# Four-layer conditioned sequence kernel: scale and shift behind the transposition, rows spread by DMA

## The chip, the cores and the metric

The kernel runs on one core of a Trainium2 chip. The metric is the device time of one execution in microseconds (us), less is better; the time of a version is the median of its timed executions.

## The reference, cut to what matters

Eight sequences of 256 tokens with 288 channels go through three transformer layers and one rotation. Every layer is conditioned: six vectors per sequence (shift, scale and gate, for attention and for the MLP) come from `silu(cond) @ W + b`. Layer 0 has a mixture of four experts as its MLP, layers 1 and 2 a plain one (288 to 1152 to 288). Layer 1's attention is between the 16 heads of one token, not between tokens.

```python
def block(x, c):                       # layers 0, 1, 2
    sh1, sc1, g1, sh2, sc2, g2 = split(silu(c) @ w_ada + b_ada, 6)
    h = layernorm(x) * (1 + sc1) + sh1
    x = x + g1 * attention(h)          # 16 heads of 18; layer 1: heads of one token attend to each other
    h = layernorm(x) * (1 + sc2) + sh2
    return x + g2 * mlp(h)             # layer 0: top 2 of 4 experts
U, _ = qr(P)                           # P is 288 x 64
R = expm(skew(silu(c) @ W.T + b))      # 64 x 64 for each sequence
x = x + ((x @ U) @ R - x @ U) @ U.T
```

## The kernel before, in words

X lies in SBUF as 16 tiles of 128 tokens x 288 channels (`X`); a block `b` is one sequence, two tiles. `XT` holds the transposed activations as fp16 pairs (high part and remainder), so that one fp32 product is seven fp16 matmuls (`PRODUCTS`, all issued by L1323). The MLP works on chunks of 512 tokens: `up_mm` has 63 matmuls of 512 columns, `down_mm` 112 of 288 columns, and an expert's weights are brought back from DRAM (`w_back`, tiles `W`, 1440 and 1368 KB) between two chunks.

A planner in Python sets the order. Generators (`prep`, `attend`, `settle_tokens`, `finish`, `householder`, `ada`, the MLP's `up` and `down`) hand out steps with `do(lane, kind, cost, ...)`; `deal` takes the line of best rank whose inputs should be ready by the planner's clock of TensorE (with the margin `SLACK`), and each engine then executes its steps strictly in that order, waiting on semaphores. `LANDS` is the time that a DMA is planned to take, `cost` that of a step; these numbers shape the order but not what hardware does. `copy` and `sooner` choose between ScalarE and VectorE, or GpSimd and VectorE. All DMAs but the loads of x are issued by SyncE (SP).

The parts that the change touches:

- **Layer norm** (`layernorm`, 48 times). VectorE makes mean and variance, GpSimd the factors, ScalarE writes z = (x - mean) * r into `YL` (`ln_z`). VectorE multiplies by the scale row (`ln_scale`, L1652), VectorE or GpSimd adds the shift row (`ln_shift`, L1657 or L2142), both rows read from `ADB`, which a DMA fills for every block with rows spread over 128 partitions. TensorE transposes (`xb_T`, L1343 and L1344), ScalarE writes the high parts (`x_hi`), VectorE the remainders (`x_lo`).
- **The QR of P** (`householder`) by 64 reflections, one after another. For each, TensorE spreads row j of `AT` over 64 partitions by an fp32 matmul with a column of the identity (`hh_mm`, L1493), ScalarE copies it into `BC` and sums its squares (`hh_row`, L2077 and L2079), GpSimd takes the root (`hh_root`, L2162), and VectorE makes ten instructions of the reflection (`hh_step`, L1857 to L1873). The line stands in the background chain `bg`, behind `ada(2)`. U is needed by the rotation after layer 2's MLP.
- **Layer 1's softmax sums** (`settle_tokens`, 8 times). VectorE takes reciprocals (`t_rec`, L1713), TensorE spreads them over partitions by 16 fp32 matmuls (`t_bc`, L1399), VectorE multiplies four times (`t_norm`, L1719) into `OT`, and `t_proj` (also L1323, tile `OT`) follows.

Of the kernel before, what the change touches and what calls it, by code (L numbers as in the profile page):

```python
# [24 lines left out]
LANDS = dict(w_back=6.0, w_keep=5.8, ad_in=3.9, ae_in=4.3, g2_in=4.0, x_in=7.5, w_in=5.0, w2_in=6.0, cond_in=5.0, tv_in=3.3)  # L25
AHEAD = 3
SLACK, BIAS = -0.3, 0.2
# [86 lines left out]
def slot(ring):  # L114
    return slots(ring, 1)


def two(ring):
    return slots(ring, 2)
# [15 lines left out]
def program(nc, I, out, scr_ada, scr_v, scr_o, scr_w1, scr_w2):  # L135
    ctx = ExitStack()
    with ctx:
# [29 lines left out]
        def mm_cost(n, cols, wide=1):  # L167
            return n * max(0.056, cols / 2350 * wide + 0.003)
# [18 lines left out]
        ADB = sb("ADB", [128, 10 * C])  # L187
        AD1 = [ADB[:, 2 * i * C:(2 * i + 2) * C] for i in range(2)]
        AD2 = [ADB[:, (4 + 3 * i) * C:(7 + 3 * i) * C] for i in range(2)]
# [7 lines left out]
        KB = [sb(f"KB{i}", [128, NH, 64], F16) for i in range(2)]  # L197
        SAME = sb("SAME", [128, 8], F16)
# [35 lines left out]
        N2 = sb("N2", [D, 2])  # L234
# [43 lines left out]
        rE, rE1, rTM, rG, rOS, rSTG = Ring([0, 1]), Ring(range(4)), Ring([0, 1]), Ring([0, 1]), Ring([0, 1]), Ring(range(7))  # L278
# [20 lines left out]
        def cond_rows(w, bias, n, dst, plus, name, wide):  # L299
            w_v = w.rearrange("(k p) n -> p k n", p=96)  # L300
            stores, total = [], n // C
            for k in range(0, total, wide):
# [17 lines left out]
                s = do(sp, "cond_out", 0.1, raises=f"os{o}", incs=16 * len(some), o=o, dst=tuple(dst[:, (k + g) * C:(k + g + 1) * C] for g in some), src=a)  # L320
                rOS.free[o] = [s]
                stores = [x for x in stores if x.sem is not s.sem] + [s]
# [5 lines left out]
        def split_cols(dst, before, w, cols, scales, bias, eager=False):  # L328
# [8 lines left out]
            for blk in range(3):  # L337
# [5 lines left out]
                for a, b, s in scales:  # L343
# [111 lines left out]
        def to_columns(b, y, full, mixed=False):  # L455
# [15 lines left out]
        def layernorm(w, L, b, sc, sh, rows, mixed=False, ask=None):  # L471
# [16 lines left out]
            while (("ada", L), 1) not in tok:  # L488
                yield "wait"
# [1847 lines left out]
```

## Time and profile before

| | |
|---|---|
| median of 3 runs | 1620.38 us (1617.28 to 1622.78) |
| profiled execution, its own time | 1614.11 us |
| span of the profiled execution | 1612.3 us |
| TensorE (PE) busy | 1391.3 us, 86% |
| VectorE (DVE) busy | 1004.1 us, 62% |
| ScalarE (ACT) busy | 787.7 us, 49% |
| GpSimd (POOL) busy | 412.9 us, 26% |
| mean granted TensorE clock | 0.94 |

PE's time is the sum of its busy time and its idle time; an idle stretch is put down to what ended it. PE is busiest, so a stage is read by asking which wait ends last on PE.

### The profile page before, as it was taken

The numbers are of one execution on the slowest core, as the hardware profiler recorded it, in microseconds if no ns is written. First come the engines' busy times: TensorE is split into PE (matmuls) and PEld (weight loads), VectorE is DVE, ScalarE is ACT, GpSimd is POOL, SyncE is SP. The second block draws the span as 40 slices with busy tenths as digits, with TensorE's granted clock in tenths as the row PEclk, the third lists the DMA queues.
The fourth block names the chain that finished last, engine by engine and source line by source line (L and its number), as shares of the span: only waits on it lengthen the run. The fifth ranks groups of instructions, "written<-read, shape, count | busy, mean of one in ns | idle before, by whom it ended". The sixth has DMA issues, their size and how long they took to land.

```text
span 1612.3 us, 30341 instructions
## 1 busy us (share of the span) xinstructions
PE 1391.3 (86%) x11814; PEld 826.6 (51%) x11814; DVE 1004.1 (62%) x2361; ACT 787.7 (49%) x1534; POOL 412.9 (26%) x551
## 2 busy tenths in 40 slices
PE   3667988988899989899898987898998899899977
PEld 1333554544455555555455554464554456565634
DVE  4676766467585666566574766856647687766442
ACT  2553545656475434454343544555444465555522
POOL 1011314133332332233231332323413131231100
PEclk9788989999999999999999999899999899999968
DMA  6232234443122210221212212230011010000010
GB/s 174 63 120 76 75 106 143 138 137 107 62 60 70 84 68 19 71 77 58 80 30 91 57 73 87 56 78 20 27 42 49 28 54 26 24 13 9 27 38 15
DMA packets 80389, 106.09 MB, mean 66 GB/s; under 512 B 39469, under 2 KB 67318, under 8 KB 76918
## 3 DMA queue, kind: packets, MB, share of 16 engines
q1 hardware_dynamic: 78134, 101.79, 20.6%
q10 hardware_dynamic: 2112, 2.36, 0.5%
q8 instruction: 94, 1.54, 0.4%
q14 instruction: 49, 0.40, 0.1%
HBM read 87.37 MB, written 16.49 MB: 64 GB/s over the span
## 4 chain that ended last, share of the span: by engine, by line
PE 51%; DVE 19%; issue 12%; DMA 6%; ACT 5%; POOL 5%; SPq 2%; POOLq 0%; DVEq 0%; ACTq 0%
PE P L1323 21%; DVE NM L1737 4%; PE P L1476 4%; PE P L1477 4%; PE P L1478 4%; PE P L1445 3%; PE P L1436 2%; PE P L1343 2%; DMA QT<-MT 1%; PE P L1412 1%; POOL N L2162 1%; POOL X L2147 1%; PE P L1333 1%; DVE AT L1869 1%; DMA STG<-in_L_b 1%
## 5 line engine op out<-in xcount | busy, mean ns | idle before, releaser
L1323 PE MATMUL P<-XT,W 128*128 128x512 f16 x1512 | 356.3, 387 | 14.4 <-DVE NM L1737 6.2
L2147 POOL TENSOR_TENSOR X<-X,TM 128x288 f32<-128x288 f32 x144 | 121.9, 847 | 716.4 <-DVE TM L1812 480.5
L1476 PE MATMUL P<-W,H 128*128 128x288 f16 x864 | 254.6, 295 | 1.9 <-POOL H L2152 1.8
L1477 PE MATMUL P<-W,H 128*128 128x288 f16 x864 | 254.1, 294 | 0.0
L1478 PE MATMUL P<-W,H 128*128 128x288 f16 x864 | 253.9, 294 | 0.0
L1323 PEld LDWEIGHTS P<-XT,W 128*128 128x128 f16 x1512 | 142.9, 99 | 193.5 <-issue 25.1
L2061 ACT ACTIVATE ARENA<-P 128x512 f32<-128x512 f32 x256 | 137.8, 602 | 131.8 <-PE P L1436 131.4
L2071 ACT ACTIVATE G<-P 128x512 f32<-128x512 f32 x216 | 128.4, 594 | 109.8 <-PE P L1323 99.9
L1737 DVE TENSOR_REDUCE NM<-P 128x2 f16<-128x512 f32 x256 | 160.3, 687 | 1.4 <-PE P L1421 0.5
L2152 POOL TENSOR_TENSOR H<-G,H 128x512 f16<-128x512 f32 x98 | 121.8, 1248 | 133.2 <-ACT H L2072 132.8
L1323 PE MATMUL P<-WQ,XT 128*128 128x288 f16 x1008 | 151.6, 303 | 4.2 <-issue 3.1
L1806 DVE TENSOR_TENSOR H<-G,H 128x512 f16<-128x512 f32 x118 | 85.4, 728 | 69.1 <-ACT H L2072 68.7
L2072 ACT ACTIVATE H<-P 128x512 f16<-128x512 f32 x216 | 128.1, 593 | 0.0
L1323 PEld LDWEIGHTS P<-WQ,XT 128*128 128x128 f16 x1008 | 97.4, 103 | 49.5 <-issue 17.9
L1476 PEld LDWEIGHTS P<-W,H 128*128 128x128 f16 x864 | 86.8, 100 | 31.0 <-issue 6.3
L1478 PEld LDWEIGHTS P<-W,H 128*128 128x128 f16 x864 | 86.9, 101 | 24.3
L1477 PEld LDWEIGHTS P<-W,H 128*128 128x128 f16 x864 | 86.9, 101 | 23.8
L1986 ACT ACTIVATE XT<-P 128x512 f16<-128x512 f32 (+1 forms) x80 | 43.5, 554 | 111.5 <-PE P L1344 111.2
L2077 ACT ACTIVATE HQS<-P 64x288 f32<-64x288 f32 (+31 forms) x64 | 24.0, 375 | 131.1 <-PE P L1493 131.1
L1812 DVE SCALAR_TENSOR_TENSOR TM<-P,CW,G 128x288 f32<-128x288 f32 x64 | 32.7, 511 | 74.3 <-PE P L1478 74.2
L1445 PE MATMUL P<-ARENA,V 128*32 128x256 f32 x1024 | 71.7, 395 | 4.7 <-ACT ARENA L2061 4.5
L1436 PE MATMUL P<-QT,KT 64*128 64x256 f16 x512 | 52.2, 285 | 24.5 <-DMA QT<-MT 22.9
(293 smaller groups left out, 2266.0 us busy)
## 6 DMA issues: line engine op xcount, KB each, us to landing
W<-scr_w SPq DMA_DIRECT2D x9, 1440.0 KB, 6.2
W<-scr_w SPq DMA_DIRECT2D x9, 1368.0 KB, 5.8
ADB<-scr_ada SPq DMA_DIRECT2D x24, 432.0 KB, 3.9
ADB<-scr_ada SPq DMA_DIRECT2D x24, 288.0 KB, 4.8
scr_w<-W SPq DMA_DIRECT2D x4, 1440.0 KB, 5.9
scr_w<-W SPq DMA_DIRECT2D x4, 1368.0 KB, 5.0
STG<-in_L_w SPq DMA_DIRECT2D x10, 432.0 KB, 3.4
STG<-in_L_w SPq DMA_DIRECT2D x7, 576.0 KB, 5.0
```

What stands on the lines that cost most here:

```text
L1323: ins = e.matmul(o, l, r, start=k == 0, stop=k == len(pairs_) - 1)
L1445: ins = e.matmul(bank(st)[32 * i:32 * i + 32, at], V32[u][:, kt, 4 * g + i, :], E32[s][:, i, kt * 256:(kt + 1) * 256], start=kt == 0, stop ...
L1476: e.matmul(o, hi, W2[:, 2 * m, :], start=False, stop=False)
L1477: e.matmul(o, hi, W2[:, 2 * m + 1, :], start=False, stop=False)
L1478: ins = e.matmul(o, lo, W2[:, 2 * m, :], start=False, stop=m == 8)
L1737: e.tensor_reduce(NM[:, :, st["par"], st["c"]], bank(st).rearrange("p (n k) -> p n k", n=2), AX.X, ALU.max, negate=True).then_inc(st.sem)
L1806: e.tensor_tensor(H[:, m, 1, :], G32[st["gi"]][:, :], H[:, m, 0, :], ALU.subtract).then_inc(st.sem)
L2061: e.activation(E32[st["s"]][:, st["h"], :], bank(st), ACT.Exp).then_inc(st.sem)
L2071: e.activation(G32[st["gi"]][:, :], bank(st), fn, scale=1.0 / WS)
L2072: e.activation(H[:, st["m"], 0, :], bank(st), fn, scale=1.0 / WS).then_inc(st.sem)
L2147: e.tensor_tensor(X[:, t, :], X[:, t, :], TM[st["k"]][:, :], ALU.add).then_inc(st.sem)
L2152: e.tensor_tensor(H[:, m, 1, :], G32[st["gi"]][:, :], H[:, m, 0, :], ALU.subtract).then_inc(st.sem)
```

## The change

Scale and shift move behind the transposition. z itself is transposed; channels are then partitions, so scale and shift are one value per partition: `full` (three instructions on ScalarE or VectorE) reads PSUM and writes `FULL`, `m_hi` makes the high part from it, `m_lo` (VectorE or GpSimd) the remainder. The values come from `SC`, which `cond_T` (three small transposes for each pair of column groups, 27 in all) and `cond_cols` fill once for every layer. The 48 loads of `ADB` become 24 loads of one gate row (`G1`). A reflection's row is spread by a DMA from SP (`hh_row`), GpSimd makes five instructions of the reflection and VectorE four; the line gets a place of its own from the start. Layer 1's reciprocals go to `RCP` and are spread by 16 DMAs from SP (`t_spread`). The remainder and the bias remainder of a weight's last rows are one instruction (`w_lo3`). The planner's constants change too. The chunks of the MLP are as before.

```diff
-LANDS = dict(w_back=6.0, w_keep=5.8, ad_in=3.9, ae_in=4.3, g2_in=4.0, ...)
-SLACK, BIAS = -0.3, 0.2
+LANDS = dict(t_spread=3.5, w_back=6.0, w_keep=5.8, g1_in=3.3, g2_in=4.0, ...)
+SLACK, BIAS = -0.41, 0.01
-            return n * max(0.056, cols / 2350 * wide + 0.003)
+            return n * max(0.058, cols / 2240 * wide + 0.003)
...
-            s = do(dve, "ln_scale", 0.76, w=w, sc=sc, src=z, rows=rows or ask())
-            r = do(lane, "ln_shift", cost, raises=f"ln_shift_{lane.name}", w=w, sh=sh, src=s)
-            yield from to_columns(b, YL[w], r, mixed)
+            m = do(pe, "xb_T", 0.8, y=YL[w], js=(j, j2), full=z, free=[pf, pf2])
+            f = copy("full", 1.1 + BIAS, 1.15, L=L, b=b, sc=sc, sh=sh, mixed=mixed, i=i, js=(j, j2), src=m, cols=cols, free=ff)
+            hi = copy("m_hi", 0.95 + BIAS, 0.75, b=b, i=i, src=f, free=before)
+            lane, cost = sooner([hi], (pool, 2.5), (dve, 1.35))
+            lo = do(lane, "m_lo", cost, raises=f"m_lo_{lane.name}", ...)
...
             r = do(dve, "t_rec", 1.75, ...)
-                    m = do(pe, "t_bc", 0.55, c=c, i=kr, j=j, src=r, free=jf)
-                    outs.append(do(dve, "t_norm", 0.6, c=c, i=raw, j=j, src=m, ...))
+            bc = do(sp, "t_spread", 0.6, incs=256, i=kr, src=r, free=ef)
+            for c in range(4):
+                outs.append(do(dve, "t_norm", 0.5, c=c, i=raw, kr=kr, rows=bc, ...))
...
-                m = do(pe, "hh_mm", mm_cost(1, C - j, 4) + 0.1, c=j, j=c, src=last, free=pf)
-                a = do(act, "hh_row", 0.55, incs=2, c=j, j=c, src=m, free=last if j else None)
-                p = do(pool, "hh_root", 0.67, src=a, half=hp)
-                d = do(dve, "hh_step", 2.3, incs=10, c=j, src=a, root=p, at=p_in)
+                r = do(sp, "hh_row", 0.1, incs=16, c=j, src=last)
+                a = do(act, "hh_norm", 0.5, c=j, src=r)
+                p = do(pool, "hh_root", 2.0, incs=5, c=j, src=a, half=hp, free=last if j else None)
+                d = do(dve, "hh_step", 1.4, incs=4, c=j, src=a, root=p, at=p_in)
...
-        bg = Line(chain(n0, ..., ada(1), ada(2), skew(), householder(), expm_steps()), 3)
+        bg = Line(chain(n0, ..., ada(1), ada(2), skew(), expm_steps()), 3)
-        deal([loads, attends, ends_, tops, preps, bg, ...])
+        deal([Line(householder(), 4), loads, attends, ends_, tops, preps, bg, ...])
...
+            def t_spread(st):
+                q.wait_ge(st["src"], st["free"])
+                for s in range(4):
+                    for c in range(4):
+                        e.dma_start(spread_of(st["i"], c)[32 * s:32 * s + 32, :], RCP[32 * s + c:32 * s + c + 1, :].unsqueeze(1).broadcast_to([1, 32, 256])).then_inc(st.sem, 16)
+            def hh_row(st):
+                q.wait_ge(st["src"])
+                e.dma_start(BC[:, c:C], AT[c:c + 1, c:C].unsqueeze(1).broadcast_to([1, D, C - c])).then_inc(st.sem, 16)
```

How the order of instructions moves is shown at three places. One reflection on VectorE, before (the first of 64; HQS holds the spread row, HS single values, TI a pivot, N a norm):

```order
L1857 ISA HQS,HS<-HQS,AT 64x288
L1857 ISA HS 64x1
L1858 TENSOR_SCALAR HS<-HQS 64x1
L1860 SCALAR_TENSOR_TENSOR HS<-HS,N 64x1
L1862 SCALAR_TENSOR_TENSOR TI<-HS,HQS,N 64x1
L1864 RECIPROCAL HS<-TI 64x1
L1865 SCALAR_TENSOR_TENSOR HS<-AT,HS 64x1
L1867 SCALAR_TENSOR_TENSOR HS<-HS,NMK 64x1
L1869 SCALAR_TENSOR_TENSOR AT<-HQS,HS,AT 64x288
L1871 SCALAR_TENSOR_TENSOR AT<-HS,AT 64x1
L1873 SCALAR_TENSOR_TENSOR AT<-IDF,HS,AT 64x1
```

And now, a reflection of length 237 with its neighbours, the reciprocals of layer 1's third block among them (RCP); six of the ten steps have gone to GpSimd or away:

```order
L1879 ISA HQS,HS<-HQS,AT 64x237
L1879 ISA HS 64x1
L1881 RECIPROCAL HS<-TI 64x1
L1883 SCALAR_TENSOR_TENSOR HS<-HS,NMK 64x1
L1885 SCALAR_TENSOR_TENSOR AT<-HQS,HS,AT 64x237
L1735 RECIPROCAL RCP<-P 128x256
```

SP's queue around a reload of layer 0's weights in the first half of layer 1, before (W<-scr_w is the reload, QT<-MT a row of maxima that the attention scores wait for):

```order
L2219 DMA W<-scr_w 128x5760 [waits s_up_mm]
L2261 DMA QT<-MT 1x16x128 [waits s_tq_dve,s_t_top_out]
L2261 DMA QT<-MT 1x16x128
L2227 DMA ADB<-scr_ada 128x864 [waits s_proj_gate,s_ln_shift_dve]
L2219 DMA W<-scr_w 128x5472 [waits s_down_mm]
```

And now: the reflections' rows (HQS<-AT) and the 16 issues of a spread (ARENA<-RCP) stand ahead of the reload and of QT<-MT:

```order
L2321 DMA HQS<-AT 64x1x251 [waits s_hh_step]
L2321 DMA HQS<-AT 64x1x250 [waits s_hh_step]
L2321 DMA HQS<-AT 64x1x249 [waits s_hh_step]
L2309 DMA ARENA<-RCP 32x1x256 [waits s_t_av,s_t_rec]
L2309 DMA ARENA<-RCP 32x1x256 x15
L2265 DMA W<-scr_w 128x5472 [waits s_down_mm]
L2303 DMA QT<-MT 1x16x128 [waits s_tq_act,s_tq_dve,s_t_top_out]
```

TensorE behind the last attention product of layer 1's third block (ARENA,V and ARENA,EV), before; the spread stands as ARENA,IDF, and the projection of OT soon behind it:

```order
L1388 MATMUL P<-ARENA,V_0 32x128 x4
L1391 MATMUL P<-ARENA,EV 32x256 x4
L1323 MATMUL P<-WQ,XT 128x288 x14
L1323 MATMUL P<-XT,W 128x512 x7
L1399 MATMUL P<-ARENA,IDF 32x256 x16
L1356 MATMUL P<-IDH,QB 64x128 x16
L1323 MATMUL P<-WP,OT 128x288 x4
L1356 MATMUL P<-IDH,KB 64x128 x16
```

And now, for the fourth block, whose projection comes soonest: ahead of the rows shown, 56 of the `down_mm` matmuls (the last one is the first row) stand between its last attention product and OT; the spread has left TensorE:

```order
L1496 MATMUL P<-W,H 128x288
L1342 MATMUL P<-XT,W 128x512 x7
L1342 MATMUL P<-WP,OT 128x288 x8
L1342 MATMUL P<-XT,W 128x512 x35
L1369 MATMUL P<-IDF,ARENA 128x128 x2
```

## Rows read from the trace of the kernel before

**Rows 1.** The page: busy time, share and instructions of each engine.

```profile
PE 1391.3 (86%) x11814; PEld 826.6 (51%) x11814; DVE 1004.1 (62%) x2361; ACT 787.7 (49%) x1534; POOL 412.9 (26%) x551
```

**Rows 2.** Stretches: length, busy (x) PE PEld DVE ACT POOL, clock, DMA share, GB/s.

```profile
0.00:200.00 200.00, 132.30 (x1095) 72.17 (x1096) 126.17 (x263) 87.61 (x162) 33.64 (x67) 0.88 0.34 101
...
400.00:1000.00 600.00, 541.63 (x4525) 323.37 (x4523) 369.84 (x1037) 281.15 (x589) 175.00 (x222) 0.98 0.21 66
1000.00:1500.00 500.00, 447.61 (x4189) 274.11 (x4189) 337.95 (x736) 263.00 (x501) 134.76 (x176) 0.94 0.12 35
```

**Rows 3.** Waits of PE: line, what it waited for, us, times, longest.

```profile
PE P L1493 <- DVE AT L1873: 33.7, 26, 4.3
...
PE P L1436 <- DMA QT<-MT: 22.9, 8, 4.1
PE P L1378 <- DMA QT<-MT: 15.0, 6, 4.8
PE P L1421 <- DVE NM L1737: 14.9, 17, 2.7
...
PE P L1323 <- DVE OT L1719: 7.6, 6, 5.4
...
PE P L1343 <- POOL ARENA L2142: 5.6, 3, 2.9
...
PE P L1343 <- DVE ARENA L1657: 3.4, 2, 2.0
```

**Rows 4.** Groups by line, the reflections: busy us, mean ns, idle before and releasers.

```profile
L2162 POOL TENSOR_TENSOR N<-N,HP 64x1 f32<-64x1 f32 x64 | 42.2, 660 | 65.1 <-ACT HQS L2079 65.0
L1493 PE MATMUL P<-AT,IDF 64*64 64x288 f32 (+42 forms) x128 | 41.7, 406 | 35.7 <-DVE AT L1873 33.7 <-DVE NM L1700 1.3 <-ACT ARENA L2061 0.6
...
L1857 DVE CUSTOM_DVE_ANT_0 HQS<-HQS,AT 64x288 f32<-64x288 f32 (+31 forms) x64 | 30.8, 482 | 21.9 <-ACT HQS L2079 21.3
...
L1860 DVE SCALAR_TENSOR_TENSOR HS<-HS,N 64x1 f32<-64x1 f32 x64 | 21.5, 336 | 28.9 <-POOL N L2162 25.8
...
L1873 DVE SCALAR_TENSOR_TENSOR AT<-IDF,HS,AT 64x1 f32<-64x1 f32 x64 | 13.5, 210 | 2.3
```

**Rows 5.** Groups by line: the spread of reciprocals and its neighbours.

```profile
L1399 PE MATMUL P<-ARENA,IDF 128*32 128x256 f32 x256 | 15.9, 383 | 1.2 <-DVE ARENA L1713 1.2
...
L1719 DVE TENSOR_TENSOR OT<-P,ARENA 128x256 f32<-128x256 f32 x32 | 15.3, 591 | 5.7 <-PE P L1399 5.5
...
L1713 DVE RECIPROCAL ARENA<-P 128x256 f32<-128x256 f32 x8 | 14.0, 1747 | 0.0
```

**Rows 6.** Groups by line: the layer norm's parts and its transposes.

```profile
L1343 PE MATMUL P<-IDF,ARENA 128*128 128x128 f32 x256 | 50.0, 291 | 16.5 <-POOL ARENA L2142 5.6 <-DVE NM L1737 4.0 <-DVE ARENA L1657 3.4
...
L2142 POOL TENSOR_TENSOR ARENA<-ARENA,ADB 128x576 f32<-128x576 f32 x32 | 48.4, 1514 | 71.3 <-DVE ARENA L1652 71.2
...
L1652 DVE TENSOR_TENSOR ARENA<-ARENA,ADB 128x576 f32<-128x576 f32 x48 | 36.9, 770 | 14.6 <-ACT ARENA L1993 10.7 <-DMA ADB<-scr_ada 3.9
```

**Rows 7.** SP's queue in order of time: start, us, DMA issues.

```profile
533.49 1.15 SPq L2261 DMA_DIRECT2D QT<-MT  x2
...
848.60 0.33 SPq L2219 DMA_DIRECT2D W<-scr_w  x1
852.18 1.14 SPq L2261 DMA_DIRECT2D QT<-MT  x2
```

**Rows 8.** The chain that ended last: start, us, piece.

```profile
144.87 1.76 DMA QT<-MT
...
518.52 1.62 PE P L1323 x7
...
537.56 0.12 PE P L1477
...
852.73 2.68 DMA QT<-MT
```

**Rows 9.** DMA issues by line: count, KB each, median us to landing.

```profile
W<-scr_w SPq DMA_DIRECT2D x9, 1440.0 KB, 6.2
```

More of the change, by code:

```diff
@@ L319, in cond_rows @@
                 yield [a]
[L320 to L322 removed]
+                last = []
+                some = [g for g in some if L is None or k + g in (2, 5)]
+                if some:
+                    last.append(do(sp, "cond_out", 0.1, raises=f"os{o}", incs=16 * len(some), o=o, gs=tuple(some), dst=tuple(dst[:, (k + g) * C:(k + g + 1) * C] for g in some), src=a))
+                    stores = [x for x in stores if x.sem is not last[0].sem] + last
+                if L is not None:
+                    yield from slot(rP)
+                    _, j, pf = rP.take()
+                    m = do(pe, "cond_T", 0.4, o=o, n=32 * len(bufs), j=j, src=a, free=pf)
+                    rOS.free[o] = last + [m]
+                    yield [m]
+                    c = do(act, "cond_cols", 0.65, L=L, k=k, n=len(bufs), j=j, src=m)
+                    rP.free[j] = [c]
+                    for g in range(len(bufs)):
+                        tok["cols", L, k + g] = c
+                else:
+                    rOS.free[o] = last
                 for g in some:
@@ L885, in finish @@
                 ot_rd[0] = ms_
[L886 to L887 removed]
+            g1_rd[u] = [v]
+            yield from layernorm(1, L, b, 4, 3)
             if L == 0:
@@ L1853, in hh_step @@
                 j = st["c"]
-                bc, aj, a1 = BC[:, j:C], AT[:, j:C], AT[:, j:j + 1]
-                nb, sg, g, rt, w, d = (HS[:, k:k + 1] for k in range(6))
-                q.wait_ge(st["src"], st["at"], (st.sem, st.first) if st.first else None)
-                e.tensor_tensor_reduce(out=HQ[:, j:C], in0=bc, in1=aj, scale=1.0, scalar=0.0, op0=ALU.mult, op1=ALU.add, accum_out=d).then_inc(st.sem)
-                e.tensor_scalar(sg, bc[:, 0:1], 0.0, 2.0, ALU.is_ge, ALU.mult).then_inc(st.sem)
@@ L1866, in hh_step @@
-                q.wait_ge(consts, st.at(6))
-                e.scalar_tensor_tensor(out=g, in0=w, scalar=rt, in1=NMK[:, j:j + 1], op0=ALU.mult, op1=ALU.mult).then_inc(st.sem)
-                q.wait_ge(st.at(7))
+                bc, aj = BC[:, j:C], AT[:, j:C]
+                g, rt, w = (HS[:, k:k + 1] for k in range(3))
+                q.wait_ge(st["src"], st["at"], st["root"].at(4), (st.sem, st.first) if st.first else None)
+                e.tensor_tensor_reduce(out=HQ[:, j:C], in0=bc, in1=aj, scale=1.0, scalar=0.0, op0=ALU.mult, op1=ALU.add, accum_out=w).then_inc(st.sem)
```

300 lines of the change are left out of this document (164 added, 136 removed).

## Prediction

> **What bounds the kernel now.** I read the page's first part, then stretches, then PE's waits, then groups by line. TensorE is busy for 1391.3 of 1612.3 us and no other engine for more than 62% [rows 1], so the time is PE's busy time plus 221.0 us of PE's idle time. The stretches say where the idle time lies [rows 2]: 67.7 of the first 200 us, 58.4 of the 600 us in which layer 0's experts run beside layer 1, 52.4 of the 500 us behind them. An engine off PE only matters where PE waits for it. The largest such waits inside the kernel are for the reflections (33.7 us in 26 waits), for the row of maxima QT<-MT that SP sends (22.9 and 15.0), for the row maxima on VectorE (14.9), for OT (7.6), and for the shift of the layer norm (5.6 and 3.4) [rows 3].
>
> **What leaves PE.** The 64 fp32 matmuls of the reflections keep PE busy for 41.7 us, and it idles 33.7 us for them, since each can only start when VectorE has finished the last reflection [rows 4]. The work goes altogether: **-41.7**. Of the waits I take **-30.0**: in a full MLP stretch the next matmul is ready, but some waits will turn into a wait for something else. Bounds: -33.7 if none does, -17 if half do. The 128 matmuls (256 in the trace) that spread the reciprocals are 15.9 us of PE [rows 5]: **-15.9**. What comes to PE is 27 small transposes; the nearest row is L1343, 50.0 us for 256 [rows 6], 0.195 us each: **+5.3** (none would be the lower bound, twice as much the upper).
>
> **The layer norm.** Before, VectorE multiplies (0.77 us) and VectorE or GpSimd adds (as much, or 1.51 us) ahead of the transposes [rows 6]. That is 1.5 to 2.3 us of latency which goes. `full` comes in behind the transposes, three instructions; the trace has none like it, and the nearest is L1719 with 0.59 us for 128x256 [rows 5], so at most 1.8 us, on VectorE 14 times and ScalarE 34 times. A layer norm's chain so changes by +0.3 us at the worst, and by about -1.1 if `full` takes 1.2. Of the 9.0 us that PE waited for the shift [rows 3] I take **-6**; bounds -9.0 and +5. VectorE is relieved on the whole: six of the instructions of a reflection, L1860 with 336 ns and L1873 with 210 among them [rows 4], are 64 x 6 x 0.21 to 0.34 = 81 to 129 us, and L1652 another 36.9 [rows 6], while part of `full` and `m_hi` comes in. With some 100 of 1004 us gone from VectorE, a third of PE's wait for the row maxima, 14.9 us [rows 3], should go: **-5** (bounds 0 and -14.9). GpSimd gets four more small instructions per reflection: at most 64 x 4 x 0.66 = 169 us by L2162 [rows 4], less the 48.4 of L2142 [rows 6]. It is 26% busy [rows 1]; that is its cover, and I put it at nothing.
>
> **The spread of the reciprocals, now on SP.** The plan counts 0.6 us for the issue of 16 DMAs and 3.5 for landing. But two SBUF-to-SBUF issues took 1.15 us [rows 7], 0.57 each, so the 16 hold SP for 9.1 us, and the last lands 1.76 later, as QT<-MT did [rows 8]: 10.9 us in place of 4.1, eight times. Then come VectorE's four products. From the last attention product to a ready OT it is 1.75 + 9.1 + 1.76 + 4 x 0.59 = 15.0 us [rows 5, 7, 8]. In PE's order 56 `down_mm` matmuls of 0.12 us and seven `up_mm` of 1.62 together stand between for the fourth block [rows 8]: 8.3 us, so PE stops for 6.7. The sixth block stands alike; together 13.4. For the third and fifth block 28 and 49 such matmuls stand between, 14.7 us, about enough; for the others more. Queued behind the stuck `t_norm` on VectorE are the remainders `h_lo` and the gates `down_gate`, for which ScalarE's gelu and PE's banks wait: I add half a microsecond a block, 4 us. Queued behind the spread on SP are reloads of W and QT<-MT. **+17**; bounds 0 (all hidden) and 87 (8 x 10.9, nothing hidden).
>
> **The rows of the reflections, now on SP.** A row costs SP 0.57 us and 1.76 to land, and a reflection's round gets longer than before (GpSimd's five in a row are up to 5 x 0.66). That alone costs nothing: 64 rounds of even 10 us are 640, the line starts at once, and U is needed only behind layer 2's first MLP chunk. What costs is the order. Each row waits on SP for VectorE's last reflection, with loads behind it; and ScalarE (`hh_norm`) and GpSimd (`hh_root`) wait in order for the row to land, with gelu and the additions to X behind them. In SP's order 13 of the 64 rows stand directly behind a reload or a save of 1.4 MB. A reload takes 6.2 us [rows 9]; QT<-MT, issued 3.6 us behind one [rows 7], landed after 2.68 rather than 1.76 [rows 8], that is, with the reload's end (848.60 + 6.2 = 854.8 against 855.4). A row issued at once behind a reload should so come 4.4 us late. 13 x 4.4 = 57 us is the upper bound; PE has up to seven other banks to fill meanwhile, so I take about a sixth: **+9** (lower bound 0).
>
> **The start.** P's load and the first rows stand in SP's queue among the first loads, with some `w_adaln` columns behind them, while the round trip of scale and shift through DRAM is gone. I see no sign of either winning and put it at nothing, within 5 us. The merged `w_lo3` lies beside other work.
>
> **The sum**, against the profiled execution's own time: 1614.1 - 41.7 - 30.0 - 15.9 + 5.3 - 6 - 5 + 17 + 9 = 1546.8 us. The median of the runs is 6.3 above that execution (1620.4), and I carry that over: **1553 us**.
>
> **The rivals.**
>
> *A: the new waits stay hidden and the old ones vanish.* The spread and the rows cost nothing, all 33.7, 9.0 and 14.9 us of waits go: 1614.1 - 41.7 - 33.7 - 15.9 + 5.3 - 9.0 - 14.9 + 6.3 = 1510 us. For it: PE has MLP matmuls in reserve in most of the 600 us stretch, where its clock is already 0.98 [rows 2]. Against it: the same was so for QT<-MT, whose waits still cost 37.9 us [rows 3], with an issue and landing only a little longer than planned.
>
> *B: the rows behind a reload cost in full.* ScalarE stops 4.4 us at each of 13 places and gelu is what PE is waiting for in an `up_mm` stretch. The sum then has 57 in place of 9: 1601 us. For it: the one crossing that rows 7 and 8 show. Against it: a reload of W1 is followed by `down_mm`, in which ScalarE has little to do.
> The Trainium skill ("DMA: Bandwidth & Descriptors", section "Queues, rings and completion order") says that on each DMA engine descriptors are consumed in ring order, which is B's mechanism; the crossing in rows 7 and 8 agrees with it, 855.4 against 854.8.
>
> *C: slower, by SP's queue.* With 192 new issues of 0.57 us, 109 us, less the 24 loads saved, SP's queue gets full, and each row in it waits for VectorE. QT<-MT, V and the reloads stand behind. Each of the 24 attentions waits for QT<-MT, and the price falls on PE at once, as rows 3 show. The gain of 67 us is used up from 67 / 24 = 2.8 us more at each; at 4 us more it is 1553 + 96 = 1649 us. Against it: most of SP's time it waits for other engines, and only 4 of the QT<-MT pairs have a reflection's row directly ahead.
>
> *D: no effect to speak of.* The 100 us off PE's path are replaced by waits of the same size, because something behind PE (the planner's order as a whole) sets the pace: 1610 to 1620 us. For it only that the order of every engine changes.
>
> **Chances.** Forecast (1525 to 1580) 0.58, A 0.18, B 0.13, C 0.06, D 0.05. The measurement can tell about 0.3%, 5 us, from no change. Faster by more than that: 0.58 + 0.18 + 0.13 + a part of D = 0.91; same 0.03; slower 0.06. The range that leaves out C, D and the outer parts of A and B is 1508 to 1600 us.
>
> **What would show it.** PE busy at about 1391.3 - 41.7 - 15.9 + 5.3 = 1339 us, VectorE near 900, GpSimd above 450. No waits of PE for reflections. On SP 16 issues in a row of about 9 us in all, and behind them PE's wait for OT of 6 to 7 us in layer 1's fourth and sixth block; a spread that takes 4 us says that this term was wrong. ScalarE idle for 4 us ahead of a reflection's squares, behind a reload, with PE idle behind it, is B. PE's wait for QT<-MT far above 37.9 us is C. The forecast is wrong, too, if PE's idle time, 221 before, isn't near 1547 - 1339 = 208 less the 2 us around the span: then a stage that I hold for unchanged, the start above all, has changed.

## The result, and the profile after

The changed kernel takes **1643.06 us** (median of 4 runs, 1641.87 to 1645.18), the kernel before 1619.84 in the same comparison: a ratio of 1.0144, with a 95% interval from 1.0123 to 1.0166. It is 1.4% slower where 1553 us was forecast. Its profiled execution has a span of 1640.2 us at a mean granted clock of 0.912, against 1612.3 us and 0.940 before.

The page's first part, which answers to [rows 1]:

```profile
PE 1326.4 (81%) x11457; PEld 811.6 (49%) x11457; DVE 872.0 (53%) x1908; ACT 816.3 (50%) x1581; POOL 426.1 (26%) x802
```

TensorE's work went down as forecast, to 1326.4 us (1339 was worked out), and VectorE's to 872.0 (near 900). GpSimd's 426.1 is less than the 450 that I had named. But the idle time of TensorE, 1640.2 - 1326.4 = 313.8 us, is 92.8 more than before, where 208 was expected. The stretches, against [rows 2]:

```profile
core 0: us, PE busy (x) PEld busy (x) DVE busy (x) ACT busy (x) POOL busy (x), PEclk, DMA share, GB/s
0.00:200.00 200.00, 122.78 (x1009) 64.98 (x1010) 127.77 (x295) 94.41 (x194) 45.31 (x124) 0.84 0.36 84
200.00:400.00 200.00, 171.47 (x1473) 103.56 (x1471) 123.64 (x270) 123.71 (x237) 66.69 (x126) 0.95 0.46 125
400.00:1000.00 600.00, 481.25 (x4472) 305.94 (x4470) 278.71 (x634) 258.84 (x515) 158.06 (x310) 0.91 0.38 60
1000.00:1500.00 500.00, 433.25 (x3641) 267.16 (x3641) 281.20 (x582) 273.44 (x509) 136.65 (x213) 0.93 0.20 39
```

In the 600 us in which layer 0's experts run beside layer 1, TensorE is busy for 481.3 us instead of 541.6: 60 us lost there. The first 200 us lost 9.5, the next 200 some 4 and the 500 from 1000 us on 14. The granted clock of the long stretch is 0.91, where it was 0.98. TensorE's waits, against [rows 3]:

```profile
engine line waited for: us in total, times, longest us
PE P L1342 <- DVE OT L1741: 109.4, 7, 19.3
PE P L1439 <- DVE NM L1759: 26.5, 14, 15.0
```

The first row alone is more than the 92.8 us by which the idle time grew: the projection of layer 1 waits for OT for 109.4 us in seven waits, up to 19.3 long, one in each of the first seven blocks. Before it was 7.6 [rows 3]. In the eighth block TensorE waits for something else, 15.0 us for the row maxima NM (the longest wait of the second row). The reason is the same, since it is VectorE that stands still. Its first product waits for the spread in every one of the eight blocks, and whatever stands behind that product in VectorE's order waits with it:

```profile
DVE OT L1741 <- DMA ARENA<-RCP: 121.5, 8, 16.6
```

The waits for the reflections (33.7) and those of layer 1's scores for QT<-MT (15.0) are gone; the other waits for QT<-MT are about as before (24.7 against 22.9).

How one such wait comes about, the first block's, is seen in three timelines (start, duration, then engine and line). SP's issues:

```profile
547.88 15.49 SPq L2309 DMA_DIRECT2D ARENA<-RCP  x16
```

VectorE's reciprocals and its first product:

```profile
545.98 1.75 DVE L1735 RECIPROCAL RCP<-P 128x256 f32<-128x256 f32 x1
...
567.69 0.59 DVE L1741 TENSOR_TENSOR OT<-ARENA 128x256 f32<-128x256 f32 x1 [15.45 <-DMA ARENA<-RCP]
```

and TensorE's projection:

```profile
570.22 4.02 PE L1342 MATMUL P<-WP,OT 128*128 128x288 f32 x8 [13.93 <-DVE OT L1741]
```

The reciprocals are ready at 547.73. SP then issues 16 DMAs for 15.49 us, 0.97 each, and the product starts at 567.69: 20.0 us for what I had put at 10.9. TensorE ran out of other work 13.93 us before the projection. What such an idle stretch does to the work behind it shows in the granted clock, third from the end in these rows of the idle stretch and of the 5 us behind it:

```profile
556.00:570.00 14.00, 0.29 (x3) 0.00 (x0) 2.31 (x5) 0.00 (x0) 0.00 (x0) 0.65 0.83 119
570.00:575.00 5.00, 4.78 (x32) 3.12 (x32) 0.97 (x3) 1.09 (x2) 0.98 (x2) 0.61 0.08 32
```

It is 0.65 on average in the idle stretch, so the lower of the two levels (1.2 GHz) was granted for most of it, and still 0.61 in the busy 5 us behind it. The eight projection matmuls there take 4.02 us; the next eight, at 579 us, take 2.21. All 128 take 48.8 us, 36.5 before:

```profile
L2020 ACT ACTIVATE FULL<-P,SC 128x256 f32<-128x256 f32 (+1 forms) x102 | 49.2, 555 | 22.6 <-PE P L1370 22.4
L1342 PE MATMUL P<-WP,OT 128*128 128x288 f32 x128 | 48.8, 545 | 109.4 <-DVE OT L1741 109.4
...
L2111 ACT ACTIVATE HQS<-HQS 64x288 f32<-64x288 f32 (+31 forms) x64 | 26.5, 414 | 222.8 <-DMA HQS<-AT 222.6
```

The other rows here are new pieces: `full` takes 0.55 us an instruction, the columns' transposes 4.0 us of TensorE in all, and ScalarE sat idle for 222.6 us ahead of the reflections' squares, waiting for rows.

The two new kinds of DMA, each with its issues and its time from issue to landing. The spread:

```profile
L2309 SPq DMA_DIRECT2D ARENA<-RCP x128: 502/1093/1395, 547.9 to 1202.4; - x128
...
DMA to landing us min/median/max: 3.3/5.5/6.9
```

The row of a reflection:

```profile
L2321 SPq DMA_DIRECT2D HQS<-AT x64: 463/484/1249, 16.8 to 1084.8; - x64
...
DMA to landing us min/median/max: 3.7/4.1/5.7
```

### The profile page after: what moved, and what is told of

The parts are those of the page before. It is cut to its first block, busy times and chain, and to the rows that moved or that the text cites. A ratio compares the mean times of both kernels' runs of the same rounds, so it can differ in the third digit from the quotient of the medians.

```text
span 1640.2 us, 29488 instructions
## 1 busy us (share of the span) xinstructions
PE 1326.4 (81%) x11457; PEld 811.6 (49%) x11457; DVE 872.0 (53%) x1908; ACT 816.3 (50%) x1581; POOL 426.1 (26%) x802
## 4 chain that ended last, share of the span: by engine, by line
PE 50%; issue 12%; DVE 9%; DMA 9%; SPq 9%; ACT 6%; POOL 4%; POOLq 0%; DVEq 0%; ACTq 0%
PE P L1342 25%; SPq L2309 7%; PE P L1494 4%; PE P L1495 4%; PE P L1496 4%; DMA HQS<-AT 4%; PE P L1463 3%; DVE NM L1759 2%; PE P L1454 2%; PE P L1369 2%; DMA ARENA<-RCP 2%; PE P L1430 2%; POOL X L2185 1%; ACT FULL L2020 1%; PE P L1359 1%
## 5 line engine op out<-in xcount | busy, mean ns | idle before, releaser
L2190 POOL TENSOR_TENSOR H<-G,H 128x512 f16<-128x512 f32 x95 | 114.9, 1212 | 165.9 <-ACT H L2106 156.9
L1342 PE MATMUL P<-WQ,XT 128*128 128x288 f16 x1008 | 144.4, 295 | 9.5 <-ACT WQ L1987 6.6
L2111 ACT ACTIVATE HQS<-HQS 64x288 f32<-64x288 f32 (+31 forms) x64 | 26.5, 414 | 222.8 <-DMA HQS<-AT 222.6
L1342 PE MATMUL P<-WP,OT 128*128 128x288 f32 x128 | 48.8, 545 | 109.4 <-DVE OT L1741 109.4
L1342 PEld LDWEIGHTS P<-WP,OT 128*128 128x128 f32 x128 | 32.0, 259 | 123.0 <-DVE OT L1741 112.3
L1439 PE MATMUL P<-KT,QT 64*128 64x256 f16 x512 | 48.2, 289 | 46.1 <-DVE NM L1759 26.5
L1879 DVE CUSTOM_DVE_ANT_0 HQS<-HQS,AT 64x288 f32<-64x288 f32 (+31 forms) x64 | 28.5, 445 | 106.1 <-POOL HQS L2206 65.3
```

The costliest lines, as they stand in the source:

```text
L1342: ins = e.matmul(o, l, r, start=k == 0, stop=k == len(pairs_) - 1)
L2190: e.tensor_tensor(H[:, m, 1, :], G32[st["gi"]][:, :], H[:, m, 0, :], ALU.subtract).then_inc(st.sem)
```

## The experiments

Each kernel is a change of the changed kernel, or of the one before, as its diff says. e1 to e4 have 1615.9 us as the kernel before's median, e5 to e8 1620.9, e9 to e12 1617.9, e13 to e16 1618.3, e17 and e18 1618.2. All ratios are against it. e14, the changed kernel with the old cost constants, gave no time.

### Which part is it (e1 to e4)

**e1**: the reciprocals go back to TensorE, all else as in the changed kernel.

```
-            bc = do(sp, "t_spread", 0.6, incs=256, i=kr, src=r, free=ef)
...
+                    m = do(pe, "t_bc", 0.55, c=c, i=kr, j=j, src=r, free=jf)
...
+                    outs.append(do(dve, "t_norm", 0.6, c=c, i=raw, j=j, src=m, ...
```

> Of the changed kernel one part is undone: the reciprocals of layer 1 are spread by TensorE's t_bc again, as before. Theory S (the spread by 16 DMAs is what was mis-sized): TensorE's 109.4 us of waits for OT fall back to about 8, and 15.9 us of t_bc come back: 1643 - 101 + 16 = 1558 us, 1545 to 1575. Theory R (the reflections' rows on SP's queue cost as much): it stays at 1600 or above, and the idle time turns up ahead of the banks that ScalarE frees. Theory T (the start and the lower clock are losses of their own): between, 1575 to 1600, with the granted clock still near 0.91.

Measured: 1557.58 us, ratio 0.9629 (0.9602 to 0.9655), within a microsecond of theory S. Its stretches and its wait for OT:

```profile
0.00:200.00 200.00, 122.02 (x1006) 64.34 (x1007) 127.11 (x293) 94.29 (x194) 45.53 (x124) 0.83 0.36 84
...
400.00:1000.00 600.00, 554.23 (x5097) 352.32 (x5095) 321.03 (x724) 291.70 (x577) 191.32 (x374) 0.97 0.29 67
```

```profile
PE P L1349 <- DVE OT L1756: 12.0, 5, 5.0
```

The 600 us stretch has 554.2 us of TensorE work again and OT costs 12.0. So the spread alone costs 1643.1 - 1557.6 = **85.5 us**, and without it the change makes the kernel faster. The start is not better: 122.0 us in the first 200, as in the changed kernel.

**e2**: of the change only scale and shift behind the transposition are left, with the merged `w_lo3` and the new cost constants (e1's diff, and with it `hh_mm`, the old `hh_row`, `hh_root` and `hh_step`, in the background line).

> Of the changed kernel only scale and shift behind the transposition is left (with the small merges that go with it); reciprocals and reflections are as before. My sum for this part was +5.3 - 6 - 5: about 1615 us, 1605 to 1620. Theory T (the layer norm's new chain and the start lose time): 1625 or above. Against e1 it gives the price of the reflections: by the sum 63 us more than e1.

Measured: 1587.61 us, 0.9815 (0.9791 to 0.9839). This part is worth 28 us, not 6, and the reflections by DMA on top of it (e1) 30, not 63. Two waits of TensorE say where some of the missing 33 us are: for QT<-MT, behind SP's queue, 42.6 us in e1 and 28.2 in e2, and for the layer norm's z from ScalarE (`xb_T` for `ln_z`), 18.6 and 5.8.

**e3**: the kernel before with the reflections' part alone.

```
-                m = do(pe, "hh_mm", mm_cost(1, C - j, 4) + 0.1, c=j, j=c, src=last, free=pf)
...
-                d = do(dve, "hh_step", 2.3, incs=10, c=j, src=a, root=p, at=p_in)
+                r = do(sp, "hh_row", 0.1, incs=16, c=j, src=last)
...
+                d = do(dve, "hh_step", 1.4, incs=4, c=j, src=a, root=p, at=p_in)
...
-        deal([loads, attends, ...
+        deal([Line(householder(), 4), loads, attends, ...
```

> The kernel before with one part of the change: the rows of the reflections by DMA, four steps on VectorE, a line of their own. Sum: 1620 - 41.7 - 30 + 9 = 1557 us (1545 to 1575) if the parts add up. Theory R (rows stuck behind reloads stop ScalarE and so TensorE): 1600 or more.

Measured: 1642.82 us, 1.0159 (1.0136 to 1.0182): slower by 27 us, though all reflections' work is off TensorE. Its first stretches:

```profile
0.00:200.00 200.00, 109.13 (x934) 59.05 (x935) 130.68 (x303) 79.64 (x168) 43.96 (x135) 0.80 0.44 100
200.00:400.00 200.00, 164.27 (x1335) 92.94 (x1334) 137.00 (x289) 107.48 (x208) 65.71 (x116) 0.91 0.44 116
```

109.1 and 164.3 us stand against 132.3 and 175.6 in [rows 2]: 34 us are lost by 400 us. The wait for the layer norm's shift (L1650) is 22.9 us, where it was 3.4 and 5.6 on its two engines [rows 3].

**e4**: the changed kernel with only the reflections undone.

> The changed kernel with only the reflections undone (by TensorE and in the background line, as before). Theory S: e2 plus what the spread costs, some 85 us net of the t_bc saved, about 1700 us. If spread and reflections hurt each other on SP's queue, it costs clearly less here than between e1 and the changed kernel: 1660 or below.

Measured: 1666.84 us, 1.0312 (1.0287 to 1.0338). Spread on top of e2 costs 79 us, on top of e1 85.5: nearly the same with and without reflections' rows on the queue. (The 1700 expected was 85 on top of the 1615 expected for e2.) But the waits for OT are only 36.2 us here, 23 more than e2's 13.3:

```profile
PE P L1514 <- DVE AT L1903: 61.1, 33, 13.8
PE P L1345 <- DVE OT L1749: 36.2, 5, 12.0
...
PE P L1433 <- DVE QB L1695: 14.3, 1, 14.3
PE P L1396 <- DVE TM L1842: 13.5, 1, 13.5
PE P L1497 <- DVE H L1836: 12.9, 1, 12.9
```

VectorE waits for the spread as long as in the changed kernel, 115.1 us in eight waits. TensorE, though, often comes first to something else that stands behind the stuck product in VectorE's order: a reflection (twice, 13.2 and 13.8 us; in e2 no wait for one is over 3.4), the queries' remainder QB, the gates' product TM, the MLP's H. So where the plan does not know the spread's length, its price is the time for which VectorE stands still, and the wait for OT is only the most frequent form of it.

### Where the reflections' rows cost (e5, e6)

Why is the start worse with them? SP's first issues in e1:

```profile
17.14 0.51 SPq L2336 DMA_DIRECT2D HQS<-AT  x1
17.69 0.59 SPq L2246 DMA_DIRECT2D H<-in_L_w_adaln  x1
...
67.12 0.75 SPq L2294 DMA_DIRECT2D QT<-MT  x1
```

and in e2:

```profile
6.38 0.42 SPq L2254 DMA_DIRECT2D H<-in_L_w_adaln  x1
...
52.25 0.74 SPq L2302 DMA_DIRECT2D QT<-MT  x1
```

In e1 the first row waits on SP for P, whose load was issued 10.5 us earlier (6.60), and the next load of `w_adaln` goes at 17.69 instead of 6.38. The later rows wait on SP for VectorE's last reflection, the third one for 21.2 us, and the load of `w_proj` behind it goes at 52.65, in e2 at 39.78. The first QT<-MT goes at 67.12 instead of 52.25. In e3 the wait for P is not what costs, since the same `w_adaln` load goes at 20.35 there and at 19.64 in the kernel before; the loads behind the later rows are late (`w_gate` at 52.04 against 34.91).

**e5**: e1 with the reflections in the background line again, their rows still by DMA.

```
-        deal([Line(householder(), 4), loads, ...
+        bg = Line(chain(..., skew(), householder(), expm_steps()), 3)
```

> e1 (TensorE spreads the reciprocals) with one more edit: the reflections, rows still by DMA, go back into the background line behind skew, so that the first row no longer waits on SP for P ahead of a load of w_adaln. Theory Q (the rows cost where they stand in SP's and ScalarE's order at the start, 15 us at the first QT<-MT and some 24 us of TensorE work by 400 us): 1557.6 less 15 to 24, 1534 to 1543 us, and the first 200 us hold about 137 us of TensorE work as in e2, not 122. Theory V (the rows cost as much anywhere): within 5 us of e1, 1553 to 1562.

Measured: 1567.07 us, 0.9672 (0.9633 to 0.9712): no better than e1, somewhat worse. Its stretches show both halves:

```profile
0.00:200.00 200.00, 135.87 (x1177) 76.19 (x1178) 129.69 (x282) 103.25 (x196) 34.46 (x73) 0.87 0.28 79
...
1500.00:1561.00 61.00, 48.60 (x486) 34.88 (x481) 24.98 (x53) 13.46 (x34) 3.18 (x4) 0.99 0.11 40
```

The start is repaired as expected (135.9 us, and 176.6 in the next 200: 21 more than e1). But reflections that start at 410 us end at 1376 and not at 1006, and the matrix exponential, a chain of small fp32 matmuls, is left for the end: 486 matmuls in the last 61 us, where e1 has 223 in its last 57. The gain is given back; that the late end is what takes it is my reading, no run changes it alone.

**e6**: the same edit to e3.

> e3 (the kernel before with the reflections by DMA) with the reflections in the background line behind skew again. Theory Q: the 23 and 11 us of TensorE work missing in the first two stretches of e3 come back and the 27 us loss turns into a gain: 1643 - 34 = 1609 or less, down to 1575. Theory V: stays at 1635 to 1650.

Measured: 1585.04 us, 0.9776 (0.9748 to 0.9805): 58 us less than e3, by moving one line of work. There the reflections' part is worth 36 us instead of costing 27.

### What the spread's price is made of (e7, e8, e17, e16)

**e7**: the same 512 rows of 1 KB in 4 DMAs instead of 16.

```
-                for s in range(4):
-                    for c in range(4):
-                        e.dma_start(spread_of(st["i"], c)[32 * s:32 * s + 32, :], RCP[32 * s + c:32 * s + c + 1, :].unsqueeze(1).broadcast_to([1, 32, 256]))...
+                for c in range(4):
+                    src = RCP[c:128:32, :].unsqueeze(1).broadcast_to([4, 32, 256])
+                    e.dma_start(spread_of(st["i"], c), src).then_inc(st.sem, 16)
```

> The changed kernel with the same bytes and the same 1 KB rows of the spread, in 4 DMAs to 128 partitions each in place of 16 to 32. Theory I (each issue costs about 1 us, 15.5 us for 16): the issues take 2 to 4 us and the last lands 5.5 later, 9 us in place of 21, and the time falls by some 70 us to about 1575. Theory P (the engines need that long for 512 rows of 1 KB out of four partitions, and the queue only holds SP back): first issue to last landing stays at 16 to 21 us, and the time at 1625 to 1645.

Measured: 1584.36 us, 0.9774 (0.9751 to 0.9797). SP's issues and VectorE's reciprocals and first product:

```profile
549.49 5.27 SPq L2309 DMA_DIRECT2D ARENA<-RCP  x4
```

```profile
547.59 1.75 DVE L1735 RECIPROCAL RCP<-P 128x256 f32<-128x256 f32 x1
...
562.13 0.59 DVE L1741 TENSOR_TENSOR OT<-ARENA 128x256 f32<-128x256 f32 x1 [8.28 <-DMA ARENA<-RCP]
```

The 4 issues take 5.3 us, not 15.5, and the product starts 12.8 us after the reciprocals (549.34 to 562.13) instead of 20.0. TensorE's wait for OT is 55.8 us. 7.2 us less in each of eight places is 58, and 59 us are gained. So theory I holds in its main part, but an issue costs 1.3 us here, and the product starts 7.4 us after the end of the issues and not 5.5. Where the time goes shows in the share that the 16 DMA engines are busy (next to last column), here in e7 between 552 and 556 us, while nothing else moves much:

```profile
552.00:556.00 4.00, 4.00 (x102) 3.27 (x101) 0.69 (x1) 2.09 (x6) 0.00 (x0) 1.00 0.23 51
```

and the same in the changed kernel:

```profile
552.00:556.00 4.00, 4.00 (x69) 3.00 (x62) 0.24 (x1) 0.48 (x3) 0.00 (x0) 1.00 0.83 29
```

With 16 DMAs the engines are busy for 0.83 and move 29 GB/s; with 4 they are busy for 0.23 and move 51. The changed kernel's DMA view of a stretch in which only a spread runs, 1146 to 1158 us, has the packets:

```profile
DMA packets 525, 0.38 MB, mean 31 GB/s; under 512 B 173, under 2 KB 524, under 8 KB 524
...
q1 hardware_dynamic: 524, 0.36, 80.0%
```

0.80 x 16 x 12 = 154 us of engine time for 351 packets of 1 KB and 173 short ones: up to 0.44 us for a packet of 1 KB. In e7's 4 us above it is 0.23 x 16 x 4 = 14.7 us for 203 packets, 0.07 us each. That issuing is slow because the engines behind it are is my reading: the shortest issue takes 0.50 us and the median 1.09, and no run separates the two. The Trainium skill ("DMA: Bandwidth & Descriptors", section "Why a DMA increments its semaphore by 16 and not by 1") says that a DMA is spread over the largest number of engines, up to 16, that divides the slowest dimension of both sides. By that rule I estimate 16 for a spread of one row to 32 partitions and 4 for e7's (4 x 32 rows to 128 partitions). The shares agree with it: 0.83, and 0.23 where 4 of 16 can give 0.25 at most. So fewer engines spread the rows faster. Why a packet out of a single partition is so slow on 16 engines is not shown by these runs.

**e8**: the changed kernel, its plan told the truth.

```
-            bc = do(sp, "t_spread", 0.6, incs=256, ...
+            bc = do(sp, "t_spread", 15.5, incs=256, ...
-LANDS = dict(t_spread=3.5,
+LANDS = dict(t_spread=5.0,
```

> The changed kernel, the same instructions, but the plan that sets the order counts 15.5 us for issuing the spread and 5 for landing (it counted 0.6 and 3.5). Theory H (it is latency that an order can hide): the waits for OT fall from 109 to under 40 us, about 1575 us (1560 to 1600). Theory N (layer 1 has too little beside the spread, and SP's loads stand behind it): 1625 or more.

Measured: 1631.32 us, 1.0068 (1.0041 to 1.0095): 12 us back of 85. VectorE no longer stands still at the product (0.8 us in all), yet TensorE still waits 56.3 us for OT, since the spread itself is as long as before, and something else stands there, too:

```profile
PE P L1342 <- DVE OT L1741: 56.3, 5, 14.9
PE P L1342 <- ACT H L2106: 30.5, 4, 14.9
```

Its origin is in SP's order at one such place:

```profile
736.45 15.41 SPq L2309 DMA_DIRECT2D ARENA<-RCP  x16
751.91 1.21 SPq L2265 DMA_DIRECT2D W<-scr_w  x1
...
756.60 9.08 SPq L2321 DMA_DIRECT2D HQS<-AT  x2
```

and in ScalarE's order:

```profile
761.92 0.41 ACT L2111 ACTIVATE HQS<-HQS 64x244 f32<-64x244 f32 x1 [22.15 <-DMA HQS<-AT]
```

VectorE ends a reflection at 741.84. Its row is queued on SP behind the spread (until 751.86), a reload, two QT<-MT and the gates' rows, goes at 756.60 and lands at 761.9. ScalarE, in order, waits for it for 22.15 us with the gelus behind, and TensorE waits 14.7 for H. That is rival B's mechanism, behind the spread instead of behind a reload.

**e17**: e4 (no reflections' rows on SP) with the plan told 14 and 5 us.

> e4 (spread by 16 DMAs, reflections on TensorE) with the plan told 14 us of issue and 5 of landing. In e8 the same truth gave the changed kernel only 12 us, and two new waits of 15 us for ScalarE's H stood behind reflection rows held up by the spread. If that coupling is what ate the gain, then here, without such rows, it is larger: 1666.8 falls by 30 us or more, to 1637 or below. If layer 1 merely has too little work beside the spread: 1650 to 1665.

Measured: 1627.57 us, 1.0060 (1.0044 to 1.0076), 39 us less than e4 and more than three times what e8 gained. That is what was expected if the coupling with the rows ate the gain in e8; since the order is another one, too, it is no proof. TensorE's waits for OT, 36.2 us in e4, are gone, and so are the single waits of 13 to 14 us for VectorE, but it still is 40 us above e2. The largest wait is that of `hh_mm` for VectorE's reflection, 60.7 us in 39 waits, none over 3.9. It was 61.1 in e4 and 30.0 in e2: with the spread the reflections are late in either plan.

**e16**: e10 (below) with e7's form of the spread, planned with 5.2 and 4.8 us.

> e10 with the reciprocals by DMA again, in 4 DMAs as in e7, and the plan told their measured 5.2 us of issue and 4.8 of landing. If a latency of 12 us in place of 20 can be hidden once it is planned for: the 16 us of t_bc are saved, 1525 to 1540. If not, waits for OT of 40 to 56 us remain as in e7: 1560 to 1580.

Measured: 1564.64 us, 0.9676 (0.9662 to 0.9691), 25.5 us more than e10. VectorE waits 37.3 us for the spread, TensorE 19.4 for OT (11.9 in e10), and QT<-MT, 32.6 us in e10, now has 64:

```profile
PE P L1456 <- DMA QT<-MT: 42.4, 11, 8.5
PE P L1406 <- DMA QT<-MT: 21.4, 4, 8.2
```

The best form of the spread that I tried, in a plan that knows it, still loses to 16 us of matmuls. The longer waits for QT<-MT, which SP issues, fit SP's queue as the reason.

### How much is the order alone (e9 to e13, e15, e18)

**e9**: e1, with the reflections in a line of their own that starts when layer 0's block 3 has its q and k.

```
             last = p_in
+            while ("qk", 0, 3) not in tok:
+                yield "wait"
             for j in range(D):
```

> e1 with the reflections in their own line as there, but the first row waits in the plan until layer 0's block 3 has its q and k. The start should be e5's (135.9 and 176.6 us of TensorE work in the first two stretches, against 122.0 and 169.4 in e1), and the reflections should still end early enough that the matrix exponential is not left for the end, as it was in e5 (486 matmuls in the last 61 us, against 223). Theory Q: e1 less the 15 to 21 us of the start, 1537 to 1546 us. Theory V (the gain at the start is given back wherever the rows run): 1553 to 1562.

Measured: 1589.50 us, 0.9831 (0.9803 to 0.9858). Neither theory: 32 us worse than e1.

**e12**: the same from block 2 on.

> As e9, but from layer 0's block 2 on: some 40 us earlier. Theory Q: within 5 us of e9, since the start has been freed by then. If rows among the weight loads of layer 0 are what costs: 5 us or more above e9.

Measured: 1548.14 us, 0.9577 (0.9553 to 0.9602): 41 us better than e9 for a start one block earlier.

**e10**: e9, and the plan counts 4.3 us for a row's landing.

```
-LANDS = dict(t_spread=3.5,
+LANDS = dict(hh_row=4.3, t_spread=3.5,
```

> e9, with the plan counting 4.3 us for a row of the reflections to land (2.2 before; the trace has 4.0). If ScalarE's and GpSimd's waits for rows in order (184 us idle on ScalarE in e1) stop work that TensorE needs, the longer figure gives better places: 5 to 10 us less than e9. If not: within 4 us of e9.

Measured: 1539.10 us, 0.9515 (0.9493 to 0.9536): 50 us better than e9, by one number in the plan, and more than the 5 to 10 expected.

**e18**: e12 with the same number.

> e12 with the plan counting 4.3 us for a row to land, as e10 does to e9 (there 50 us less). If the longer figure is what helps: 10 us or more below e12's 1548, near 1535. If e9 was only an unlucky order: within 8 us of e12.

Measured: **1511.43 us**, 0.9342 (0.9316 to 0.9367), 37 us better than e12. The number helps at both places. What it does shows in ScalarE's waits for rows. e9 and, with the number, e10:

```profile
ACT HQS L2128 <- DMA HQS<-AT: 181.7, 36, 10.8
```

```profile
ACT HQS L2128 <- DMA HQS<-AT: 96.0, 18, 8.2
```

e12 has 170.1 us in 36 waits, and with the number, e18:

```profile
ACT HQS L2128 <- DMA HQS<-AT: 104.6, 19, 11.0
```

36 waits become 18 or 19, and their time falls from 170 to 182 us to about 100. The rows land after 4.0 us in all four. A plan that knows this seems to put other work of ScalarE ahead of an instruction that waits for a row, so that half of the waits are gone. e18 is the fastest version found, 6.6% below the kernel before. Its TensorE is busy for 1326.2 us, as long as the changed kernel's though it spreads the reciprocals as well (at a mean granted clock of 0.948 against 0.912), and idle for 1510.7 - 1326.2 = 184.5. Of the 600 us stretch it is busy for 561.1, at a clock of 0.98:

```profile
400.00:1000.00 600.00, 561.11 (x5157) 359.74 (x5158) 322.16 (x713) 294.87 (x580) 182.08 (x355) 0.98 0.31 73
```

**e11**: e2 with the plan's cost constants of the kernel before (slack, bias, the prices of a matmul and of `o_T`, MLP pieces, L3_WT's columns).

```
-SLACK, BIAS = -0.41, 0.01
+SLACK, BIAS = -0.3, 0.2
-            return n * max(0.058, cols / 2240 * wide + 0.003)
+            return n * max(0.056, cols / 2350 * wide + 0.003)
```

> e2 (scale and shift behind the transposition alone) with the plan's cost constants as in the kernel before (slack, bias, price of a matmul, price of o_T, MLP pieces, two columns groups at a time for L3_WT). If e2's 28 us come from the layer norm and the missing round trip through DRAM: 1580 to 1596. If they come from the constants: 1605 to 1618.

Measured: 1567.14 us, 0.9687 (0.9665 to 0.9710), 20 us better than e2, below the range of either case.

**e13**: the kernel before with the changed kernel's constants.

> A control: the kernel before, not one operation changed, only the plan's cost constants (slack, bias, price of a matmul and of o_T, MLP pieces, L3_WT three at a time) as in the changed kernel. Theory K (the order alone moves the time by tens of us, so differences of 20 us between single kernels are no price of an operation): away from 1618 by 15 us or more, rather slower, 1635 to 1650, if the constants cost e2 the 20 us that e11 got back. Theory L (they only suit one kernel or the other): within 8 us.

Measured: 1616.59 us, 0.9987 (0.9971 to 1.0003): no difference. **e15**: e10 with the old constants.

> e10, the fastest so far, with the constants of the kernel before. Theory K: anything from 1515 to 1565, since another order is drawn. Theory M (the old constants are better throughout): 20 us less than e10, 1515 to 1525.

Measured: 1539.51 us, 0.9516 (0.9500 to 0.9532): none against e10 either. So the constants are no better or worse as such; one kernel of three lands 20 us elsewhere with them. What they do to the changed kernel itself stays open (e14).

## Why the prediction was wrong, point by point

The step that failed is **the spread of the reciprocals**. I put "The spread of the reciprocals, now on SP" at +17 us, and saved 15.9 of `t_bc`: +1 together. e1 measures +85.5 (e4 against e2: +79). That one term turns 67 us of forecast gain into 23 us of loss; without it, e1, the kernel takes 1557.6 us. That this is only 5 from the forecast is luck: the layer norm gave 22 us more than forecast and the reflections 33 less. As I had written the term, before `t_bc`'s 15.9 are taken off, it measured 85.5 + 15.9 = 101 us, outside my bounds of 0 to 87. What was mis-sized in it:
- The issue. I took 0.57 us each from QT<-MT [rows 7], 9.1 for 16. They take 15.5, 0.97 each. QT<-MT was a pair, not a train of 16, and carries 4 KB, not 32.
- The landing. I took 1.76 us from QT<-MT [rows 8]. It is 5.5 (median), and 4.1 for a row of the reflections.
- So it is 20.0 us and not 10.9, some 9 us more to cover at each of eight places: 72 us. The upper bound was too low for the same reason: it counted eight times 10.9.
- The cover, the MLP matmuls that stand between in TensorE's order. In the fourth and sixth block I expected waits of 6.7 us, and they are 18.4 each; in the third and fifth, where 14.7 us of cover should have been about enough, they are 12.5 and 12.2. In the first, second and seventh I had expected more than enough. But when their reciprocals were ready, TensorE had 8.6, 5.6 and 7.6 us of work left, and the waits are 13.9, 19.3 and 14.6. I counted from the last attention product; in the second block VectorE came to the reciprocals only 10.6 us after that product's end (601.94 against 591.4), with other work ahead of them in its order, and the cover ran off meanwhile.
- What stands behind the stuck `t_norm` on VectorE. I gave it half a microsecond a block. VectorE stood still for 121.5 us in all, and in the eighth block (15.0 us for NM) and in e4 (five waits of 12.9 to 14.3 us) that is what TensorE waited for.
- A cost that I did not have at all: the clock. Waits of 12 to 19 us bring TensorE's granted clock down, and the work behind them runs slowly: 48.8 us for the projection's matmuls against 38.3 in e1 and 36.5 before.

**The reflections off TensorE** (-41.7, -30.0, +9, together -63). The busy time and the waits went as said, and yet e1 against e2 shows -30 and e3 against the kernel before +27. The step that failed is "That alone costs nothing ... the line starts at once". Starting at once costs 21 to 34 us of TensorE's work by 400 us (e1 against e5, e3 against the kernel before), because rows that wait on SP for P or for VectorE's last reflection hold up the loads behind them. ScalarE, too, waits in order for rows that land after 4 us, not the planned 2.2 (51.2 us by 400 us in e1); how the loss divides between the two was not separated. I had put **the start** at nothing "within 5 us"; it was 9.5 us of TensorE's work in the first 200. With a later start and the true landing in the plan (e18 against e2) the part is worth 76 us, more than forecast, though some of that can be the luck of one order.

**The layer norm** (+5.3, -6, -5: together -6). e2 shows -28, e11 -51 with other constants. The transposes take 4.0 us and `full` 1.65 for three instructions, both as worked out. What I missed may be what else waited for the longer chain and for the round trip through DRAM. TensorE was idle for 14.4 us ahead of the up-projection's matmuls before and for 2.8 in e2, and e2's first 200 us hold 136.9 us of work, where it was 132.3 [rows 2]:

```profile
0.00:200.00 200.00, 136.89 (x1188) 77.23 (x1189) 129.73 (x282) 103.50 (x196) 34.56 (x73) 0.87 0.29 80
```

Waits for QT<-MT fell from 37.9 [rows 3] to 28.2, and those for `w_adaln`'s columns from 23.4 to 18.3. How much of the 28 is the operations and how much the order stays open: e11 shows that another order of the same operations moves it by 20.

**The rivals.** C had the sign and, by luck, the size (1649 us), but not the place: QT<-MT costs 24.7 us in the changed kernel, less than the 37.9 before, and what SP's queue delays is the spread itself. C's place shows in e1 and e3, where QT<-MT has 42.6 and 47.8 us. B (rows stuck in SP's queue stop ScalarE and gelu) is real in e8, behind the spread, but in the changed kernel TensorE waits less than 2 us for the gelu's H, though ScalarE is idle for 222.6 us ahead of the squares. It was priced at 57 us for reloads only. A and D fell.

**The chances.** 0.06 for slower was too little for a change that makes 192 new issues on an in-order queue and whose price came from another kind of DMA. I had the spread's upper bound at 87 and let the range end at 1600, where the sum with that bound is 1553 + 70 = 1623.

## What to carry to other kernels

A DMA that replaces a matmul for spreading rows over partitions costs its issues, one after another on an in-order queue, all that stands behind them there, and all that stands behind the first instruction that waits for them on its own engine; price it by the rows, sources and DMAs it has, not by the nearest small one, and take the bound where nothing like it is in the trace. In a kernel whose order comes from a plan, one wrong duration (2.2 us for 4.0) cost 37 to 50 us: measure a new operation's landing first, and put it into the plan before judging the change. And judge a change in more than one order: the same instructions took 1511 to 1590 us here (e1, e5, e9, e10, e12, e18), so 20 us between two single kernels are no price of an operation. The spread's 79 and 85 are no larger than that range; they hold because the trace shows the waits they are made of, at every one of the eight places.

## What the runs showed of the hardware

- Sixteen DMAs that each spread one 1 KB row to 32 partitions go at one per 0.97 us and about 30 GB/s, with the 16 DMA engines busy for 0.83 (changed kernel). The same bytes in four DMAs move at 51 GB/s at a share of 0.23 (e7).
- A row of up to 1152 bytes that goes to 64 partitions lands after 4.1 us (median of 64, changed kernel), 2.3 times QT<-MT's 1.76 [rows 8].
- Over 14 us in which TensorE is busy for 0.29 its mean granted clock is 0.65, over the busy 5 us behind them 0.61. Eight fp32 projection matmuls directly behind such a wait take 4.02 us, the next eight 2.21 (changed kernel).
